# Gathering neighbour rows once per tile of 128 edges, into a ring, in all four edge stages

## The chip, the cores and the metric

The kernel runs on one core of a Trainium2 chip. The metric is the device time of one execution in microseconds (us), as the median of several runs. The engines are PE (TensorE; its weight loads are a row of their own, PEld), DVE (VectorE), ACT (ScalarE), POOL (GpSimd) and SP (SyncE, which only issues transfers and semaphore operations here). They run side by side and wait for each other by semaphores.

## What is computed

A graph of 12,500 nodes with 64 channels and 200,000 edges `src -> dst`, sorted by `dst`. Two CG convolutions, a layer norm, then two graph attention (GAT) convolutions, a batch norm behind each and a layer norm at the end, all in float32:

```python
def _cgconv(x, edge_index, Wf, bf, Ws, bs):
    z = concatenate([x[i], x[j]], axis=-1)          # i = dst, j = src
    m = sigmoid(z @ Wf + bf) * softplus(z @ Ws + bs)
    return x + segment_sum(m, i, num_segments=n)
...
def gat_conv(x, src, dst, edge_attr, W, We, att_s, att_d, att_e, bias):
    xl = x @ W                                      # self loops are added
    alpha = leaky_relu(a_src[src2] + a_dst[dst2] + a_edge, 0.2)
    ex = exp(alpha - segment_max(alpha, dst2)[dst2])
    p = ex / segment_sum(ex, dst2)[dst2]
    return segment_sum(xl[src2] * p[..., None], dst2) + bias
```

`dst` is drawn as the square of a uniform number, so that nodes with a low number have many edges and the last ones about 8 each.

## The kernel before, in words

**Tiles, blocks, steps.** The edges are cut into 1,563 tiles of 128, the nodes into 98 blocks of 128. A tile whose edges end in several blocks is visited once for each. Such a visit (tile, block) is a **step**: 1,658 steps are needed, padded to 1,664. Four steps are a **group** (416 groups), 128 steps a **batch** (13 batches, 32 groups each). `setup` works out which tile and which block each step has, and brings the edges' data into step order.

**Four edge stages.** `cg_edges` runs twice, `gat_edges` twice; between them stand `cg_tables`, `cg_finish`, `gat_tables` and `gat_finish`, each ended by a barrier of all engines. In an edge stage POOL gathers for each step the 128 source rows of its tile with one indirect DMA (`indirect_dma_start`; L677 for CG, from `q_table`, 128 words a row; L1134 for GAT, from `xl_table`, 65 words a row). Its loop is a fixed order of 1,664 gathers a stage, with one wait every four.

**CG.** For each group PE adds the gathered rows (L774, one 128x512 product with the identity) to the rows of the destination's table, which it picks with a one-hot matrix (L777, four products), and PE later sums the messages by destination (L787, four products). ACT works out logarithms and exponentials (L742 to L755), DVE the one-hot matrices (L577, L698), the messages and the accumulation (L724). The gathered rows stand in a ring of 4 groups, and POOL may refill a group when PE has done L777 on it.

**GAT.** Here POOL fills two buffers of a whole batch (128 rows of 65 words for each edge lane). Before a batch's messages can be weighed, its 128x128 scores must be complete: DVE adds the gathered score column, read with a strided view from the buffer, to the destination's part (L1189), which needs the whole batch landed; then come the segment maxima, their carries and the exponentials. This work on batch b+1 is laced into the 9 iterations (4 groups each) of the sums of batch b: the scores stand after iteration 1 on DVE (iteration 5 for the last batch). The sums are ACT's weighing (L1328, L1330), PE's products with the one-hot matrix (L1405) and DVE's accumulation (L1265). PE also spreads destination values two batches ahead (L1358, with the one-hot made by DVE in L1156 from `rel_rows`). SP fetches `rel_rows` for a pair of groups at a time (L655, L1105).

**The last batch.** When batch 11's sums reach iteration 5, DVE waits for batch 12's rows; its own sums then follow with no gather beside them.

## Time and profile before

| | us |
|---|---|
| median of 3 runs | 11,049.12 (11,041.77 to 11,055.13) |
| span of the profiled execution, first to last instruction | 9,392.2 |
| median less span: what lies around the span | 1,656.9 |

The page of the profile gives the span of the profiled execution and not its whole time, so what lies around the span is the difference to the median. The parts of the page show busy time by engine, the span in 40 slices, the costliest groups of instructions and what ended the idle time before them; the timeline shows single instructions with the engine's idle time before them in square brackets. A matmul of float32 stands as two records.

### The profile page before, as it was taken

Reading aid. Unit: us, or ns where it says so; the run is one execution under the profiler, and the core shown is the slowest. Engines: PE = TensorE matmul, PEld = TensorE weight load, DVE = VectorE, ACT = ScalarE, POOL = GpSimd, SP = SyncE. Lnnn points to the kernel's source line nnn. Section 1 sums busy time; section 2 is a strip of 40 time slices with the busy share of each in tenths; the row PEclk is TensorE's granted clock in tenths of the full one; section 3 lists DMA queues with packets and bytes.
Section 4 is the critical chain, followed back from the end, with each engine's and each line's share of the span. In section 5 each row is a group of like instructions: output and inputs, shape, how many; then the busy total and the mean of one; then the engine's idle time right before and its main releaser. Section 6 shows DMA issues by size and latency. Waiting matters only on the chain. (4 is left out here: it accounts for less than half of the span.)

```text
span 9392.2 us, 131283 instructions
## 1 busy us (share of the span) xinstructions
PE 5120.9 (55%) x26955; PEld 4302.7 (46%) x26956; DVE 4670.8 (50%) x14160; ACT 3046.4 (32%) x8219; POOL 6571.9 (70%) x6801
## 2 busy tenths in 40 slices
PE   2677777777677777777533253434552234343444
PEld 1555555555555555555423243434542234343443
DVE  6555555555555555555623353434552235353546
ACT  0444444444444444444302122222320122121222
POOL 2777777777577777777557777777716777777771
PEclk6888787788778887887655555555555555555555
DMA  4322223222222232222232232222203223222221
GB/s 134 91 76 77 76 75 76 75 77 77 82 77 77 75 76 77 77 75 76 68 76 53 45 59 50 56 52 52 49 11 75 45 49 59 46 58 49 58 44 30
DMA packets 436755, 612.92 MB, mean 65 GB/s; under 512 B 180134, under 2 KB 217754, under 8 KB 434779
## 3 DMA queue, kind: packets, MB, share of 16 engines
q0 software_dynamic: 214032, 332.71, 17.2%
q1 hardware_dynamic: 217116, 262.20, 10.3%
q10 hardware_dynamic: 5193, 13.44, 0.4%
q8 instruction: 144, 2.36, 0.1%
q14 instruction: 270, 2.21, 0.1%
HBM read 575.04 MB, written 32.78 MB: 65 GB/s over the span
## 5 line engine op out<-in xcount | busy, mean ns | idle before, releaser
L677 POOL DMA_INDIRECT big<-q_table,idx_stage x3328 | 3279.5, 985 | 1007.8 <-issue 930.3
L1134 POOL DMA_INDIRECT big<-xl_table,idx_stage x3328 | 3199.1, 961 | 1007.9 <-issue 985.3
L1405 PE MATMUL bank<-msg,onehot 128*128 128x66 f32 x6656 | 1597.3, 424 | 2227.4 <-DVE wide L1265 2003.0
L1405 PEld LDWEIGHTS bank<-msg,onehot 128*128 128x128 f32 x6656 | 1480.8, 328 | 2276.9 <-issue 2186.1
L774 PE MATMUL bank<-big,ident 128*128 128x512 f32 x1664 | 1216.8, 821 | 1236.0 <-DMA big<-q_table,idx_stage 1145.6
L777 PEld LDWEIGHTS bank<-big,wide 128*128 128x128 f32 x6656 | 1217.7, 257 | 574.9 <-issue 574.9
L777 PE MATMUL bank<-big,wide 128*128 x6656 | 1208.0, 342 | 0.0
L577 DVE TENSOR_TENSOR onehot<-iota,dst_rel 128x512 f32<-128x512 f32 x1664 | 1145.7, 689 | 2.9 <-issue 2.9
L705 DVE SCALAR_TENSOR_TENSOR work<-bank,work 128x256 f32<-128x256 f32 x832 | 352.3, 423 | 1459.7 <-ACT work L747 1456.2
L742 ACT ACTIVATE work<-bank 128x512 f32<-128x512 f32 x832 | 496.2, 596 | 1783.4 <-PE bank L777 1781.1
L1265 DVE TENSOR_TENSOR wide<-wide,bank 128x66 f32 x3328 | 739.4, 222 | 553.8 <-issue 182.6
L787 PEld LDWEIGHTS bank<-msg,onehot 128*128 128x128 f32 x6656 | 997.1, 229 | 4.3 <-DVE msg L713 3.9
L787 PE MATMUL bank<-msg,onehot 128*128 128x67 f32 (+1 forms) x6656 | 995.6, 302 | 3.9 <-DVE msg L713 2.4
L1189 DVE TENSOR_TENSOR work<-big,onehot_t 128x128 f32<-128x128 f32 x26 | 9.9, 379 | 1879.5 <-DMA big<-xl_table,idx_stage 1879.5
L724 DVE TENSOR_TENSOR wide<-wide,bank 128x67 f32 (+1 forms) x3328 | 735.3, 221 | 364.0 <-DVE wide L724 15.3
L774 PEld LDWEIGHTS bank<-big,ident 128*128 128x128 f32 x1664 | 297.7, 224 | 1338.4 <-DMA big<-q_table,idx_stage 691.2
L1328 ACT ACTIVATE msg<-work 128x8 f32<-128x8 f32 x448 | 94.5, 211 | 1533.6 <-PE bank L1405 1532.3
L747 ACT ACTIVATE work<-work 128x512 f32<-128x512 f32 x832 | 523.6, 629 | 103.4
L744 ACT ACTIVATE work<-work 128x512 f32<-128x512 f32 x832 | 523.7, 629 | 26.7
L1358 PEld LDWEIGHTS bank<-spread_bf,big 128*128 128x128 bf16 x3328 | 347.6, 147 | 340.3 <-issue 329.1
L1328 ACT ACTIVATE msg<-big 128x8 f32<-128x8 f32 x384 | 80.9, 211 | 1277.7 <-PE bank L1405 1258.8
L1330 ACT ACTIVATE msg<-big,work 128x64 f32<-128x64 f32 x1792 | 470.3, 333 | 0.0
(216 smaller groups left out, 4138.3 us busy)
## 6 DMA issues: line engine op xcount, KB each, us to landing
wide<-rel_rows SPq DMA_DIRECT2D x416, 256.0 KB, 3.4
big<-rel_rows SPq DMA_DIRECT2D x416, 256.0 KB
big<-q_table,idx_stage POOLq DMA_INDIRECT x3328
big<-xl_table,idx_stage POOLq DMA_INDIRECT x3328
q_table<-wide SPq DMA_DIRECT2D x12, 1024.0 KB, 5.2
edge_rows<-big SPq DMA_DIRECT2D x25, 257.0 KB, 6.6
xl_table<-big SPq DMA_DIRECT2D x12, 520.0 KB, 6.7
big<-in_edge_attr ACTq DMA_DIRECT2D x6, 1024.0 KB
```

The costliest lines, as they stand in the source:

```text
L577: return nc.vector.tensor_tensor(to, k.iota[:, :].unsqueeze(1).broadcast_to([P, GROUP, P]), k.dst_rel[:, ds(s, GROUP)].unsqueeze(2).broadc ...
L677: pool.indirect_dma_start(out=ring[:, u, s % GROUP, :], out_offset=None, in_=k.q_table, in_offset=bass.IndirectOffsetOnAxis(ap=k.idx_stage ...
L724: nc.vector.tensor_tensor(to, to, agg[c % UNROLL][:, i * P:i * P + width], ALU.add).then_inc(s_add if i < GROUP - 1 else s_acc, 1)
L742: nc.scalar.activation(soft[:, j], pre[j], ACT.Abs).then_inc(s_act, 1)
L744: nc.scalar.activation(soft[:, j], soft[:, j], ACT.Exp, scale=-1.0).then_inc(s_act, 1)
L747: nc.scalar.activation(soft[:, j], soft[:, j], ACT.Ln, bias=1.0).then_inc(s_ln, 1)
L774: nc.tensor.matmul(k.psum[j][:, :], k.ident[:, :], ring[:, j].rearrange("p i c -> p (i c)"), start=True, stop=False)
L777: last_one = nc.tensor.matmul(k.psum[j][:, i * P:(i + 1) * P], turned[:, j, i, :], p_tab[:, ds(at[i], 2 * C)], start=False, stop=i == GROU ...
L787: last_one = nc.tensor.matmul(agg[j][:, i * P:i * P + width], k.onehot[:, j, i, :], k.msg[:, j, i, 0:width], start=True, stop=True)
L1134: pool.indirect_dma_start(out=buf[p][:, s, :], out_offset=None, in_=k.xl_table, in_offset=bass.IndirectOffsetOnAxis(ap=k.idx_stage[:, s:s ...
L1265: nc.vector.tensor_tensor(to, to, sum_bank[c % UNROLL][:, i * P:i * P + C + 2], ALU.add).then_inc(e_add if i < GROUP - 1 else e_acc, 1)
L1405: last_one = nc.tensor.matmul(sum_bank[c % UNROLL][:, i * P:i * P + C + 2], k.onehot[:, c % UNROLL, i, :], k.msg[:, c % UNROLL, i, 0:C + 2 ...
```

## The change

Each edge tile is gathered once, and not once per step. A stage now gathers 1,568 tiles (392 groups of 4; `TGROUPS`) and POOL writes them in tile order into a **ring**: 32 tiles for CG, 256 for GAT. Which slot a step reads is no longer fixed in the code. `setup` makes three tables in `offsets`: the ring slot of each step (`RING_ROW`; GAT's is kept in DRAM until `gat_tables`), the tile group that each step group needs (`NEED_ROW`), and for each tile group the last step group that reads it (`LAST_ROW`). Engines read them into registers with `load_values`.

SP becomes a **relay**: in tile order it waits until the readers are done with an older group (`s_used`), raises `s_free`, waits for the group's landing and raises `s_land`. POOL waits for `s_free` (in GAT also for `s_land`), PE for `s_land`. The fetch of `rel_rows` moves from SP to ACT. The indices are no longer brought into step order. In CG the identity product is split into four of 128 columns, each with a slot from a register. In GAT the score column can't be read with one strided view any more; PE copies it with 128 products of the identity by one column (`far_scores`), before DVE's scores, and ACT reads each slot by a register.

```diff
+TGROUPS = 8 * -(-TILES // (8 * GROUP))
+TAIL_TILES = TGROUPS * GROUP - TILES // P * P
+LANES = 8
...
+CG_RING = 32
+GAT_RING = 2 * P
+AHEAD = 4
...
             for row, width in ((ACC_ROW, AW), (TAB_ROW, 2 * C), (SPREAD_ROW, 2 * PARTS)):
-                link(nc.vector.tensor_scalar(k.offsets[row:row + 1, :], b_row, float(NB - 1), float(width), ALU.min, ALU.mult))
+                link(nc.vector.tensor_scalar(k.offsets[row:row + 1, 0:STEPS], b_row, float(NB - 1), float(width), ALU.min, ALU.mult))
+            link(nc.vector.tensor_scalar(clipped, b_row, float(NB - 1), None, ALU.min))
+            link(nc.vector.tensor_tensor(tile_int, iota_s[0:1, :], clipped, ALU.subtract))
+            link(nc.vector.tensor_scalar(k.offsets[RING_ROW:RING_ROW + 1, 0:STEPS], tile_int, CG_RING - 1, 7, ALU.bitwise_and, ALU.logical_shift_left))
+            link(nc.vector.tensor_scalar(gat_ring, tile_int, GAT_RING - 1, None, ALU.bitwise_and))
+            nc.vector.tensor_scalar(gat_ring, gat_ring, float(TW), None, ALU.mult).then_inc(s_ring, 1)
...
+def relay(k, sp, s_used, s_land, s_free, depth, row_base):
+
+
+    def turn(it, freeing):
+        before = it * LANES + (AHEAD - depth)
+        if any(freeing):
+            last = load_values(k, sp, LAST_ROW, before + (STEPS + freeing.index(True)), freeing.count(True), 1, GROUPS)
+        for j in range(LANES):
+            if freeing[j]:
+                sp.wait_ge(s_used, last[j - freeing.index(True)])
+                sp.sem_inc(s_free, 1)
+            sp.wait_ge(k.rows[j], it * (16 * GROUP) + (16 * GROUP + row_base))
+            sp.sem_inc(s_land, 1)
...
-                        wait(pool, s_X, b * BGROUPS + (s // GROUP - UNROLL + 1))
+                        wait(pool, s_free, b * BGROUPS + (g - CG_DEPTH + 1))
...
+                    slot = load_values(k, pe, RING_ROW, step, GROUP, 0, (CG_RING - 1) * 2 * C)
+                    need, = load_values(k, pe, NEED_ROW, it * CG_UNROLL + (STEPS + c), 1, 1, TGROUPS)
+                    pe.wait_ge(s_land, need)
                     wait(pe, s_softs, n[c - 3])
-                    nc.tensor.matmul(k.psum[j][:, :], k.ident[:, :], ring[:, j].rearrange("p i c -> p (i c)"), start=True, stop=False)
+                    for i in range(GROUP):
+                        nc.tensor.matmul(k.psum[j][:, i * P:(i + 1) * P], k.ident[:, :], ring[:, ds(slot[i], 2 * C)], start=i == 0, stop=False)
...
             if layer == 0:
+                sp.dma_start(k.offsets[RING_ROW:RING_ROW + 1, 0:STEPS], k.gat_ring_row).then_inc(s_ring, 16)
+                sp.wait_ge(s_ring, 16)
...
                     if s % GROUP == 0:
...
+                        wait(pool, s_free, b * BGROUPS + (g - GAT_DEPTH + 1))
                         pool.sem_inc(s_turn, 1)
...
+                        wait(pool, s_land, b * BGROUPS + (g - LANES + 1))
...
-                for half in range(2):
-                    v.wait_ge(s_gat[p][half], turn * (16 * HALF) + (16 * HALF + gat_base[p][half]))
-                link(nc.vector.tensor_tensor(x3[:, 0, :], gather[:, :, C], near_sb[:, :, 0], ALU.add))
+                v.wait_ge(s_far, b + 1)
+                link(nc.vector.tensor_tensor(x3[:, 0, :], k.psum[5][:, 0:P], near_sb[:, :, 0], ALU.add))
...
+            def fetch(pair, q):
+                wait(act, a_T, 2 * (pair - PAIRS) + 2 if not isinstance(pair, int) or pair >= PAIRS else 0)
+                act.sem_inc(s_fetch, 1)
+                act.dma_start(rel_pair[q], rel_row(k, pair)).then_inc(s_rel[q], 16)
...
+                        slot = load_values(k, act, RING_ROW, b * P + s, GROUP, 0, (GAT_RING - 1) * TW)
...
+                            last_one = nc.scalar.activation(k.msg[:, c, i, 0:C], ring[:, ds(slot[i], C)], ACT.Copy, scale=wsw[p][:, s + i, 0:1])
...
+            def far_scores(b):
+                wait(pe, s_fe, 2 * b)
+                for c in range(0, BGROUPS, 2):
+                    slot = load_values(k, pe, RING_ROW, b * P + c * GROUP, 2 * GROUP, 0, (GAT_RING - 1) * TW)
+                    need, = load_values(k, pe, NEED_ROW, b * BGROUPS + (STEPS + c + 1), 1, 1, TGROUPS)
+                    pe.wait_ge(s_land, need)
+                    for i in range(2 * GROUP):
+                        at = c * GROUP + i
+                        last_one = nc.tensor.matmul(k.psum[5][:, at:at + 1], k.ident[:, :], ring_score[:, ds(slot[i], 1)], start=True, stop=True)
+                last_one.then_inc(s_far, 1)
...
                 for it in range(BIT + 1):
                     sums(it, it == 0, it == BIT)
+                    if not ends(b) and it == (5 if late(b) else 1):
+                        far_scores(b + 1)
```

Three places show what stands on the engines. First PE in a CG stage, a group's forming (ISA rows are register work for an address). Before, from the end of one group's sums on (L583 loads offsets, L774 is the identity product, L777 the one-hot products):

```order
L583 TENSOR_LOAD offsets
L774 MATMUL bank<-big,ident 128x512 [waits cge0_soft_s,rows3]
L777 ISA [waits cge0_onehot_t]
L777 MATMUL bank<-big,wide 128x128
L777 ISA
L777 MATMUL bank<-big,wide 128x128
```

Now, from the same point on (L622 is the old load, L630 the new ones, L851 the split identity product):

```order
L622 TENSOR_LOAD offsets
L630 TENSOR_LOAD offsets x2
L851 ISA [waits cge1_soft_s,cge1_landed]
L851 MATMUL bank<-wide,ident 128x128
L851 ISA
L851 MATMUL bank<-wide,ident 128x128
L851 ISA
L851 MATMUL bank<-wide,ident 128x128
L851 ISA
L851 MATMUL bank<-wide,ident 128x128
L854 ISA [waits cge1_onehot_t]
```

Two register loads are added ahead of the wait for the rows, and one product became four with a register address each; the one-hot products follow as before.

Second PE in a GAT stage between iterations 1 and 2 of a batch's sums. Before, the spreading of a group (L1358) is followed directly by the next group's sums (L1405):

```order
L1358 ISA
L1358 MATMUL bank<-spread_bf,big 128x6
L70 REGISTER_ALU
L1405 MATMUL bank<-msg,onehot 128x66 [waits gat0_e_e_acc,gat0_e_e_onehot,gat0_e_e_msg]
L1405 MATMUL bank<-msg,onehot 128x66 x3
```

Now the first of 16 blocks of `far_scores` stands there (L1440 is the spreading, L1457 the product by one column):

```order
L1440 ISA
L1440 MATMUL bank<-spread_bf,big 128x6
L79 ISA
L630 ISA [waits gat0_e_factor]
L630 TENSOR_LOAD offsets
L630 ISA
L630 TENSOR_LOAD offsets
L1457 ISA [waits gat0_e_landed]
L1457 MATMUL bank<-big,ident 128x1
L1457 ISA
L1457 MATMUL bank<-big,ident 128x1
```

Between two groups of PE's sums stand 128 products, 32 register loads and 16 waits for landings; the sums come behind them.

Third ACT in a GAT stage, the weighing of a group (L1328 and L1330 before). Before:

```order
L1328 ACTIVATE msg<-big 128x4x2 [waits gat0_e_e_agg]
L1330 ACTIVATE msg<-big 128x64 x4
L1328 ACTIVATE msg<-big 128x4x2 [waits gat0_e_e_agg]
L1330 ACTIVATE msg<-big 128x64 x4
L1328 ACTIVATE msg<-big 128x4x2 [waits gat0_e_e_agg]
```

Now (L1369 is the fetch of `rel_rows`, every second group):

```order
L1399 ACTIVATE msg<-big 128x64
L1369 DMA big<-rel_rows 128x1024 [waits gat0_e_a_onehot_t]
L630 TENSOR_LOAD offsets
L1397 ACTIVATE msg<-big 128x4x2 [waits gat0_e_e_agg]
L1399 ISA
L1399 ACTIVATE msg<-big 128x64
```

ACT gained a register load and four register addresses for each group, and for each second group a transfer with a wait for DVE's one-hot.

## Rows read from the trace of the kernel before

**Rows 1.** The page: span, part 1, PEclk in 40 slices

```profile
span 9392.2 us, 131283 instructions
PE 5120.9 (55%) x26955; PEld 4302.7 (46%) x26956; DVE 4670.8 (50%) x14160; ACT 3046.4 (32%) x8219; POOL 6571.9 (70%) x6801
...
PEclk6888787788778887887655555555555555555555
```

**Rows 2.** Page part 5: count, busy us, mean ns, idle us before

```profile
L677 POOL DMA_INDIRECT big<-q_table,idx_stage x3328 | 3279.5, 985 | 1007.8 <-issue 930.3
L1134 POOL DMA_INDIRECT big<-xl_table,idx_stage x3328 | 3199.1, 961 | 1007.9 <-issue 985.3
```

**Rows 3.** Lines L677 and L1134, POOL: duration min/median/max ns, first and last start

```profile
L677 POOL DMA_INDIRECT big<-q_table,idx_stage x3328: 940/946/3329, 254.2 to 4621.6; - x196
L1134 POOL DMA_INDIRECT big<-xl_table,idx_stage x3328: 940/945/1458, 4745.8 to 9178.2; - x196
```

**Rows 4.** Timeline, POOL: first and last gather of GAT stage 1

```profile
4745.75 0.97 POOL L1134 DMA_INDIRECT big<-xl_table,idx_stage  x1 [0.81 <-POOL idx_stage L1136]
...
6855.73 0.94 POOL L1134 DMA_INDIRECT big<-xl_table,idx_stage  x1 [0.31 <-issue]
```

**Rows 5.** Timeline, PE: a CG group at the low, then at the high clock

```profile
2003.54 2.07 PE L774 MATMUL bank<-big,ident 128*128 128x512 f32 x2 [2.05 <-DMA big<-q_table,idx_stage]
2005.40 1.81 PE L777 MATMUL bank<-big,wide 128*128 x8
...
2008.64 1.12 PE L774 MATMUL bank<-big,ident 128*128 128x512 f32 x2 [0.59 <-DMA big<-q_table,idx_stage]
2009.60 1.05 PE L777 MATMUL bank<-big,wide 128*128 x8
```

**Rows 6.** Timeline, DVE: waits for a batch's rows, batches 2, 10, 11, 12

```profile
5233.08 0.38 DVE L1189 TENSOR_TENSOR work<-big,onehot_t 128x128 f32<-128x128 f32 x1 [76.71 <-DMA big<-xl_table,idx_stage]
...
6532.05 0.38 DVE L1189 TENSOR_TENSOR work<-big,onehot_t 128x128 f32<-128x128 f32 x1 [66.56 <-DMA big<-xl_table,idx_stage]
...
6693.93 0.38 DVE L1189 TENSOR_TENSOR work<-big,onehot_t 128x128 f32<-128x128 f32 x1 [67.77 <-DMA big<-xl_table,idx_stage]
...
6858.67 0.38 DVE L1189 TENSOR_TENSOR work<-big,onehot_t 128x128 f32<-128x128 f32 x1 [39.18 <-DMA big<-xl_table,idx_stage]
```

**Rows 7.** Line L583, PE's register loads: duration ns min/median/max

```profile
L583 PEldq TENSOR_LOAD <-offsets x1664: 326/332/517, 260.2 to 9085.6; - x185
```

**Rows 8.** CG, GAT stage 1: us, PE PEld DVE ACT POOL busy, PEclk, DMA

```profile
254.00:2420.00 2166.00, 1543.06 (x7488) 1203.33 (x7488) 1234.69 (x3747) 985.16 (x2081) 1643.73 (x1690) 0.81 0.29 76
...
4746.00:6859.00 2113.00, 819.20 (x4852) 786.44 (x4852) 834.41 (x2801) 453.39 (x1943) 1607.52 (x1690) 0.50 0.27 53
```

**Rows 9.** Timeline, PE: products by one column in GAT stage 1

```profile
6881.41 0.58 PE L1381 MATMUL bank<-ones_row,big 1*128 1x1 f32 x2
6881.86 0.56 PE L1382 MATMUL bank<-ones_row,big 1*128 1x1 f32 x2
```

**Rows 10.** Timeline, PE: the stop in batch 10's sums

```profile
6698.84 1.52 PE L1405 MATMUL bank<-msg,onehot 128*128 128x66 f32 x6 [72.68 <-DVE wide L1265]
```

**Rows 11.** Line L655, SP's transfers: issue to landing

```profile
DMA to landing us min/median/max: 3.0/3.4/4.3
```

**Rows 12.** Timeline, DVE in setup: the step tables; POOL's first gather there

```profile
48.40 1.88 DVE L390 TENSOR_TENSOR wide<-wide 1x1664 f32<-1x1664 f32 x1
50.31 3.12 DVE L393 TENSOR_SCALAR offsets<-wide 1x1664 int32<-1x1664 f32 x3
...
83.80 5.97 POOL L268 DMA_INDIRECT wide<-edge_rows,work  x1 [78.70 <-DMA edge_rows<-big]
```

**Rows 13.** Lines L961 and L520: duration ns min/median/max; window of L961's stage

```profile
L961 PE MATMUL bank<-gw,work x392: 417/418/477, 4702.6 to 7059.4; 64*128 64x66 f32 x196
L520 PE MATMUL bank<-small,work x784: 271/272/579, 215.5 to 2462.4; 64*128 64x128 f32 x196
...
4700.00:4745.00 45.00, 36.12 (x245) 30.75 (x245) 13.52 (x32) 12.66 (x27) 0.24 (x1) 0.50 0.57 88
```

More of the change, by code:

```diff
@@ L586, in load_offsets, with load_values @@
     return values
+def load_values(k, eng, row, first, count, low, high):
+    _, values = k.nc.values_load_multi_w_load_instructions(
+        k.offsets[row:row + 1, ds(first, count)], engines=[eng.engine], min_val=low, max_val=high,
+        skip_runtime_bounds_check_because="setup makes them so")
+    return values
+def relay(k, sp, s_used, s_land, s_free, depth, row_base):
[9 more added lines that the diff above has]
+            sp.sem_inc(s_land, 1)
+    whole = -(-(depth - AHEAD) // LANES)
+    for it in range(whole):
+        turn(it, [it * LANES + j >= depth - AHEAD for j in range(LANES)])
+    with sp.Fori(whole, TGROUPS // LANES) as it:
+        turn(it, [True] * LANES)
 def counts(eng, first, lo, hi):
@@ L637, in cg_edges @@
     at = CG_PAIRS * GROUP * P
[L638 removed]
+    ring = k.wide[:, at:at + CG_RING * 2 * C]
     soft = k.work[:, 0:UNROLL * GROUP * P].rearrange("p (u i c) -> p u i c", u=UNROLL, c=2 * C)
@@ L649, in _, with batch @@
             k.clear_old(sp)
-            def fetch(it):
-                for q in range(CG_PAIRS):
-                    wait(sp, s_T, (it - 1) * CG_UNROLL + 2 * q + 2 if not isinstance(it, int) or it else 0)
-                    sp.sem_inc(s_turn, 1)
-                    sp.dma_start(rel[q], rel_row(k, it * CG_PAIRS + q)).then_inc(s_rel[q], 16)
-            fetch(0)
-            with sp.Fori(1, CG_ITERS) as it:
-                fetch(it)
+            relay(k, sp, s_X, s_land, s_free, CG_DEPTH, row_base)
         @block.gpsimd
         def _(pool):
-            def batch(b):
-                for s in range(P):
-                    u = s // GROUP % UNROLL
+            def batch(b, tiles):
+                for s in range(tiles):
+                    g = s // GROUP
                     if s % GROUP == 0:
-                        wait(pool, s_X, b * BGROUPS + (s // GROUP - UNROLL + 1))
+                        wait(pool, s_free, b * BGROUPS + (g - CG_DEPTH + 1))
                         pool.sem_inc(s_turn, 1)
-                    if s % HALF == HALF // 2:
+                    if s % HALF == HALF // 2 and tiles == P:
                         start = b * P + (HALF if s < HALF else P)
@@ L758, in iteration @@
                     stages(u, first, last, (3, sigmoids), (2, logs))
-            pipelined(act, CG_ITERS, iteration)
+            for q in range(CG_PAIRS):
+                fetch(q, q)
+            iteration(0, True, False)
+            with act.Fori(1, CG_ITERS - 1) as it:
+                iteration(it, False, False)
+            iteration(CG_ITERS - 1, False, False)
+            iteration(CG_ITERS, False, True)
         @block.tensor
@@ L1349, in batch @@
                     weights(b + 1, 1 - p)
-            over_batches(act, batch)
+            for pair in range(BGROUPS // 2 + PAIRS):
+                fetch(pair, pair % PAIRS)
+            batch(-1, 1, -1)
+            batch(0, 0, 0)
+            with act.Fori(0, OUTER - 2) as j:
+                batch(j * 2 + 1, 1, j)
+                batch(j * 2 + 2, 0, j + 1)
+            for b in range(NBATCH - 4, NBATCH):
+                batch(b, b % 2, b // 2)
         @block.tensor
```

158 lines of the change are left out of this document (90 added, 68 removed).

## The prediction

> **What bounds the kernel now.** I read the page first: POOL is busiest with 70% of the span, the others lie at 32 to 55% [rows 1]. Then POOL's gathers. In each edge stage it issues 1,664 of them; the idle time before them, 1,007.8 us over 3,328, is 0.303 us each, put down to its own issuing, and no wait: POOL is back to back [rows 2]. A gather's median is 945 to 946 ns [rows 3], with the dispatch 1.249 us. The mean is 985 ns in CG and 961 ns in GAT [rows 2]: 0.040 and 0.016 us more each, or 67 and 27 us a stage, which comes and goes while POOL waits for nobody. GAT stage 1 shows the sum: first gather at 4,745.75, last at 6,855.73, which is 2,110.0 us, or 1.268 us a gather [rows 4].
>
> Everybody else waits for the rows. In CG, PE's idle time before L774 is ended by the gather (2.05 and 0.59 us in two groups) [rows 5]. In GAT, DVE stands still 66.6 to 76.7 us in each batch before L1189, until a batch's rows are there [rows 6]. Neighbouring batches lie 161.9 us apart (6,532.05 to 6,693.93), of which 67.8 is that wait: the work between two landings takes 94.1 us, at most 97 in other batches. The last one differs: from 6,693.93 to 6,858.67 is 164.7 us with a wait of only 39.2, so its work is 125.6 us, since the scores stand later in the sums there. So GAT has 66 us of slack in most batches and 39 in the last.
>
> **What the change removes.** 96 gathers a stage (1,664 less 1,568) at the median pitch of 1.249 us: 119.9 us. I take the median and not the mean, because I leave the 67 and 27 us of longer gathers in the stage: the other engines' work is still 1,664 steps. Of the 392 tile groups the readers need 391 (1,563 tiles), so the last group's four gathers, 5.0 us, fall beside other work.
>
> **CG, two stages.** PE gets two more register loads per group, 0.33 us each [rows 7], and four register addresses. They stand ahead of the wait for the rows, where PE idles anyway. A group of steps takes 4 x 1.289 = 5.16 us now and would take 119.9 / 416 = 0.29 less, 4.87 us. The split product moves the same columns; one-hot products of that shape take 1.05 us a group of four at the high clock against 1.12 for the one wide product, 1.81 against 2.07 at the low one [rows 5]: no loss, taken at nothing. ACT and DVE are busy for 0.46 and 0.57 of the stage [rows 8], so 6% more speed is there; ACT's transfer per two groups is hidden by its idle half. POOL's ring is deeper (8 groups, not 4) and the relay lets it run ahead of the readers, so I book no stall. The relay's own handing on I book at 0.5 us once, at the end. Saving: 119.9 + 5.0 - 0.5 = 124.4 us a stage, **249 us** for both. Bounds: 0 (PE can't follow, below) and 125.
>
> **GAT, two stages.** Added on PE are 128 products by one column a batch. The nearest rows are one-column products: L1381 starts at 6,881.41, L1382 at 6,881.86 [rows 9], 0.45 us; the eight records of L1405 and L777 at the low clock go at 0.213 us each, two records a product, 0.427 us, and I take that: 128 x 0.427 = **54.6 us a batch**. At the high clock the pitch of L777's records is 0.11 us (1.05 us for eight, with the tail) [rows 5], which gives 28.5 us: the lower bound. The register loads (32 a batch, 0.33 us [rows 7]) and the addresses run in PE's sequencer ahead of the array; I take them as hidden behind the products, and the upper bound has them in series.
>
> Where does this lie? PE reaches `far_scores` one group (about 2.2 us) ahead of the stop that starts now at 6,698.84 - 72.68 = 6,626.16 [rows 10], and DVE can't go on without it. Most of the 128 products find their rows landed and fill the stop. So a batch now lasts the longer of two things: its gathers, or 94 to 97 us of old work plus 54.6 less 2.2, about 147.6 us. The sorted `dst` of the inputs gives the tiles that each batch of steps ends on: 127, 253, 378, 501, 624, 745, 865, 985, 1,103, 1,220, 1,337, 1,453, 1,562. At 1.268 us a tile a batch takes 161 us at first and 147 to 148 us in batches 9 to 11: the gathers still win, by a hair. Scores of batch 11 then start 1,453 x 1.268 + 3 (landing [rows 11], a transfer from another queue) + 3.4 (the last 8 products) + 1 = 1,850 us into the stage. For the last batch the work is 125.6 - 2.2 + 54.6 = 178 us, while its 110 tiles take 140: here **the work wins**, and batch 12's scores start at 2,028 us. Before, that was 6,858.67 - 4,745.75 = 2,112.9 [rows 4, 6]. Saving 85 us a stage where the gathers alone would give 124; the other 39 us are the new products with no cover. The sums of batch 12 behind it are unchanged but for ACT's register loads, which its waits for PE hide; I book 1 us. So 84 us, **168 us** for both.
>
> ACT now waits with each second group for DVE's one-hot (L1156) before it issues the fetch of `rel_rows`. Behind it on ACT stands the next group's weighing, for which PE waits. DVE accumulates four groups late, so this costs ACT its lead and not the pace: nothing. POOL's second wait per group falls into the 0.30 us of dispatch: nothing, with 0.1 us x 392 = 39 us a stage as the other bound.
>
> **Setup and tables.** DVE's table chain gets five operations over 1,664 elements of one partition: one like L390 (1.88 us) and four like L393 (3.12 / 3 = 1.04) [rows 12], 6.0 us, and about eight short ones, 3 us. Everything behind them in setup hangs on DVE (POOL's first gather waits 78.7 us for its stores [rows 12]): 9 us, nothing hides it. The ring table goes out to DRAM and comes back, each 3.0 to 3.4 us [rows 11], of which the return is bare: 3 us. Together **12 us** lost (bounds 5 and 20).
>
> **Sum.** -249 - 168 + 12 = -405 us on the profiled execution's span: 9,392 to 8,987. The page doesn't show that execution's whole time; what lies around the span is taken as it was, 1,656.9 us, so the median goes from 11,049.1 to **10,644 us**.
>
> [...] The loads: the rows show 0.33 us for a register load of four values. [...]
>
> **Rivals.**
> 1. *The products are slow (slower than before).* If a register load or address can't run ahead of the array, each of the 16 blocks costs 3.4 us of products plus two loads (0.66), eight addresses and a wait, some 2.0 us: 87 us a batch instead of 54.6. Then the work wins from batch 2 on (at 488 us): 488 + 9 x (95 - 2.2 + 87) + (123.4 + 87) = 2,317 us for batch 12's scores, 204 us later than before in each GAT stage. Median 10,644 + 2 x 288 = 11,220. It decides from F, the cost of a batch's `far_scores`: the start is 1,447 + 10 F, so a GAT stage gains nothing from F = 67 us on (median 10,812), and the whole change nothing from F = 78. For it: nothing in the trace has two loads among products. Against: L583's loads run while products of the group before are under way.
> 2. *The high clock comes.* F = 28.5 us: batch 12's scores at 1,848 + 123.4 + 28.5 = 2,000 us, 28 us a stage better: 10,588.
> 3. *CG's readers can't follow.* At the low clock a CG group costs PE three times 1.7 to 1.9 us, 5.2 us, more than the 4.87 that the gathers would leave; at the high clock 2.9. The granted clock is 0.81 [rows 8], so both occur. If the shorter waits don't bring the high clock more often, or relay and loads add to each group, CG keeps its time: 10,644 + 249 = 10,893, or part of the way.
> 4. *The change saves gathers but no time*, since SP's in-order relay releases rows later than POOL can deliver them, in all stages: 11,060. Against: SP has two waits a group and nothing else to do.
>
> **Chances.** Forecast 0.53; rival 1 in full 0.09; GAT gains next to nothing (F 62 to 72) 0.11; rival 2 0.12; rival 3 0.12; rival 4 0.03. The range from 10,560 (all gathers covered, 10,563) to 10,830 (GAT stages gain nothing, plus the bounds of setup) leaves out rivals 1 and 4 and the full form of 3. About 0.2% is what a measurement of this kernel can tell from no change: faster by more 0.88, within 0.03, slower 0.09.
>
> **What would show it.** 1,568 gathers a stage, pitch 1.27 to 1.29 us, idle before each still 0.30. CG windows about 124 us shorter. In GAT, L1457's records at 0.21 us; DVE's wait for `far_scores` in each batch; batches 149 to 161 us apart and the last about 178. Wrong would be: waits ahead of POOL's gathers, a GAT batch longer than 165 us, L1457 at another pitch, or PE waiting for `s_land` in CG with the rows long there.

## The result and the profile after

The changed kernel takes **12,258.42 us** (median of 4 runs, 12,256.23 to 12,263.07) against 11,045.44 us before (median of 4, 11,038.50 to 11,055.13): ratio 1.110, 95% interval 1.108 to 1.111. The forecast was 10,644 us, faster by 4%. Direction and size are wrong.

The page of the kernel after, its span, TensorE's row of part 1, and the granted clock in 40 slices:

```profile
span 12256.2 us, 173779 instructions
PE 6901.5 (56%) x38616; PEld 6518.7 (53%) x38617; DVE 4643.4 (38%) x14173; ACT 3046.5 (25%) x8220; POOL 6237.3 (51%) x6409
...
PEclk6777777777777777755555555555555555555555
```

POOL was busy for 70% of the span before [rows 1] and is for 51% now. The span also tells something on its own: it is 2 us shorter than the time of its execution (12,258.15). Before, span and time were 1,657 us apart.

What ended POOL's idle time before its gathers, in the attention stages (L1200) and in the convolution stages (L736); the columns are us in total and how many times:

```profile
L1200 POOL DMA_INDIRECT big<-xl_table,idx_stage x3136: 938/944/1482, 5370.1 to 11913.3; - x196
...
  SPq L648: 1940.4, 120
  issue: 1028.3, 2972
```

```profile
L736 POOL DMA_INDIRECT wide<-q_table,idx_stage x3136: 938/944/4581, 255.4 to 5231.0; - x196
...
  issue: 877.8, 2783
  SPq L646: 821.2, 351
```

Before, POOL waited for nobody [rows 2]. Now it waits for the relay on SP 1,940 us in the attention stages and 821 us in the convolution stages. A gather itself still takes 944 ns, where [rows 3] has 945 to 946. The relay is only the messenger (L648 raises a landing, which SP reaches only after L646). Its own waits before L646, where it hands a freed group on, were ended by the readers, above all by ACT's last reading of a group in the attention stages (L1399) and by PE's last product on one in the convolution stages (L854); "remote" is a release whose sender the trace doesn't name (waits of SP in the kernel after; us in total, times, longest):

```profile
SPq L646 <- ACT msg L1399: 4113.6, 365, 130.1
SPq L646 <- remote: 3141.0, 350, 24.4
SPq L646 <- PE bank L854: 1381.7, 358, 14.9
```

Two starts of the first score operation in the timeline of DVE in the kernel after (start, us, and in brackets the idle time before and what ended it):

```profile
6410.10 0.29 DVE L1253 TENSOR_TENSOR work<-bank,near_sb 128x128 f32<-128x128 f32 x1 [56.32 <-PE bank L1457]
...
6656.58 0.29 DVE L1253 TENSOR_TENSOR work<-bank,near_sb 128x128 f32<-128x128 f32 x1 [74.74 <-PE bank L1457]
```

These rows answer to [rows 6]. Two batches are 246.5 us apart, where the forecast had 149 to 161. DVE waits 74.7 us of them for `far_scores` (L1457), and 171.8 us go into the rest, where [rows 6] gave 94. Over batches 2 to 11 of both stages the means are 245.9 us, of which 59.6 are that wait and 186.4 the rest. The 128 products themselves stand in 54.7 to 54.8 us in 11 of the 26 batches, as forecast, and are drawn out to as much as 83.5 us in others. The larger surprise is the work around them, which takes nearly twice its time.

A hint of why stands in the timeline of PE in a convolution stage of the kernel after:

```profile
1438.83 0.83 PE L854 MATMUL bank<-big 128*128 x6
1440.63 0.27 PE L854 MATMUL bank<-big 128*128 x1 [0.96 <-issue]
1441.36 0.36 PE L854 MATMUL bank<-big 128*128 x1 [0.47 <-issue]
1442.78 1.09 PE L864 MATMUL bank<-msg,onehot 128*128 128x67 f32 x8 [1.06 <-issue]
```

In the middle of a group, with nothing to wait for, PE goes over to one array operation in 0.7 us and back. From 750 to 2,250 us this happens close to a hundred times, and PE's idle time before its products that is put down to "issue" adds up to 467 us there, against 8 us in the same window of a2_after_u16 (an experiment below). Register operations show the same on other engines. Counted over all of the trace's records, the register, branch and semaphore operations that took 650 to 760 ns (their median is 17 to 57 ns, by engine) are:

```
kernel, its time            PE   ACT    DVE    SP   POOL
before,  9,391 us            3     0      0     0      0
after*,  9,009 us            4     0      0     0      0
before*, 11,083 us         307     0  1,872   634      0
after,  12,258 us          559   838  1,101   118      0
```

The first three rows are runs of the experiments below (e0_before, a2_after_u16, b10_before_bursts); the star marks kernels that differ slightly from the two compared. The profile shown ahead of the prediction has 3, 0, 0, 0, 0, like the first row.

### The profile page after: what moved, and what is told of

It is laid out like the page before. It is cut to its first block and busy times, and to the rows that moved or that the text cites. A ratio compares the mean times of both kernels' runs of the same rounds, so it can differ in the third digit from the quotient of the medians.

```text
span 12256.2 us, 173779 instructions
## 1 busy us (share of the span) xinstructions
PE 6901.5 (56%) x38616; PEld 6518.7 (53%) x38617; DVE 4643.4 (38%) x14173; ACT 3046.5 (25%) x8220; POOL 6237.3 (51%) x6409
## 3 DMA queue, kind: packets, MB, share of 16 engines
q0 software_dynamic: 201536, 312.86, 11.7%
## 5 line engine op out<-in xcount | busy, mean ns | idle before, releaser
L1200 POOL DMA_INDIRECT big<-xl_table,idx_stage x3136 | 2999.0, 956 | 3031.4 <-SPq L648 1940.4
L736 POOL DMA_INDIRECT wide<-q_table,idx_stage x3136 | 3131.9, 999 | 1700.7 <-issue 877.8
L851 PE MATMUL bank<-wide,ident 128*128 x6656 | 1370.2, 343 | 992.1 <-issue 959.6
L851 PEld LDWEIGHTS bank<-wide,ident 128*128 128x128 f32 x6656 | 1133.8, 243 | 1113.8 <-issue 1099.5
L1457 PE MATMUL bank<-big,ident 128*128 x6656 | 1425.6, 350 | 195.4 <-issue 187.9
L1457 PEld LDWEIGHTS bank<-big,ident 128*128 128x128 f32 x6656 | 1431.6, 332 | 190.0 <-issue 189.7
L854 PE MATMUL bank<-big 128*128 x6656 | 1238.6, 334 | 374.9 <-issue 371.3
L854 PEld LDWEIGHTS bank<-big 128*128 128x128 f32 x6656 | 1119.2, 246 | 418.8 <-issue 417.8
L1440 PEld LDWEIGHTS bank<-spread_bf,big 128*128 128x128 bf16 x3328 | 346.4, 140 | 1184.9 <-issue 1177.5
L1440 PE MATMUL bank<-spread_bf,big 128*128 x3328 | 318.3, 178 | 1160.2 <-issue 972.4
L1222 DVE TENSOR_SCALAR big<-big,iota_col 128x512 bf16<-128x512 bf16 x832 | 310.9, 378 | 1029.0 <-issue 336.2
```

The costliest lines, as they stand in the source:

```text
L736: pool.indirect_dma_start(out=ring[:, s % CG_RING * 2 * C:(s % CG_RING + 1) * 2 * C], out_offset=None, in_=k.q_table, in_offset=bass.Indir ...
L851: nc.tensor.matmul(k.psum[j][:, i * P:(i + 1) * P], k.ident[:, :], ring[:, ds(slot[i], 2 * C)], start=i == 0, stop=False)
L854: last_one = nc.tensor.matmul(k.psum[j][:, i * P:(i + 1) * P], turned[:, j, i, :], p_tab[:, ds(at[i], 2 * C)], start=False, stop=i == GROU ...
L1200: pool.indirect_dma_start(out=ring[:, slot * TW:(slot + 1) * TW], out_offset=None, in_=k.xl_table, in_offset=bass.IndirectOffsetOnAxis(ap= ...
L1440: last_one = nc.tensor.matmul(near[:, ds(column + (c * GROUP + i) * SLOT, 2 * PARTS)], turned[:, c % UNROLL, i, :], spread_bf[:, ds(at[i], ...
L1457: last_one = nc.tensor.matmul(k.psum[5][:, at:at + 1], k.ident[:, :], ring_score[:, ds(slot[i], 1)], start=True, stop=True)
```

## Experiments

Sums of stages are from the first gather of one stage to the first of the next. In all but one version of the changed kernel a mask of ten bits is laid over each value that an engine waits for (`need & 1023`, `last[...] & 1023`), one register operation more for each wait.

**Where the 1,657 us lie** (e0_before, no edit).

> The kernel before, unchanged. Its profiled span was 9,392.2 us while its runs take 11,038 to 11,055; the changed kernel's span (12,256.2) and its time (12,258.2) differ by 2 us. Theory A (the 1,657 us lie outside the span, before the first or after the last instruction): the span comes out at 9,392 again. Theory B (the profiled execution of before ran under other conditions than its timed ones): the span comes out near 11,045, and its trace shows where the 1,653 us stand.

Measured: 9,391.17 us with a span of 9,389.4. Neither theory had it: the span is 9,390 again, but so is the time. On this chip the kernel before takes 9,391 us, and 1.8 us lie around the span. So the profile shown ahead of the prediction and the runs shown with it (11,049) are of two conditions in which the same program takes different times. The text calls them two kinds of chip; whether it is the chip or something that comes and goes on one, no run here tells, since no chip was seen in both. All comparisons below are therefore with before on the same chip.

**Parts of the change, one at a time.** e1_before_pe_loads, with the load of one value beside that of four:

```diff
+ load_offsets(k, pe, TAB_ROW, ..., GROUP, 2 * C)
+ load_offsets(k, pe, TAB_ROW, ..., 1, 2 * C)
- nc.tensor.matmul(k.psum[j][:, :], k.ident[:, :], ring[:, j]...)
+ for i in range(GROUP):
+     nc.tensor.matmul(k.psum[j][:, i * P:(i + 1) * P], k.ident[:, :], ring[:, j, i, :], start=i == 0, stop=False)
```

> The kernel before with what the change adds to TensorE in the convolution stages alone: two more register loads per step (of four values and of one) and the identity product of 512 columns as four of 128. Nothing is left out. Theory 1 (TensorE's instruction stream, 164 records between two stalls in the trace of after, is what makes the convolution stages longer): both stages grow, by up to the 297 us each by which the stages of after are longer than those profiled before; 11,045 + up to 594. Theory 2 (the relay on the sync engine holds GpSimd back): no change, 11,045 within 0.3%.

Measured: 9,378.35 against 9,385.36. The values of the added loads are not used, and the trace has no load more than before (1,664 on TensorE): what ran is the split product alone (4,992 matmul records more), and it costs nothing that a single run can show. e2 and e3 are single runs too.

e2_before_act_fetch: `fetch` of the relative positions in ScalarE's program, as in the diff of the change, and none on SyncE.

> The kernel before with the fetches of the relative positions issued by ScalarE, as in the changed kernel, in all four edge stages. Nothing is left out. If the fetch's place is a cause, the time rises by 50 us or more; the prediction's own step (hidden, at nothing) says 11,045 within 0.3%.

Measured: 9,385.41 against 9,385.36. The place of the fetch costs nothing.

e3_after_cg_whole:

```diff
- slot = load_values(k, pe, RING_ROW, step, GROUP, 0, (CG_RING - 1) * 2 * C)
- for i in range(GROUP):
-     nc.tensor.matmul(..., k.ident[:, :], ring[:, ds(slot[i], 2 * C)], start=i == 0, stop=False)
+ nc.tensor.matmul(k.psum[j][:, :], k.ident[:, :], p_tab[:, 0:GROUP * 2 * C], start=True, stop=False)
```

> The changed kernel with a mask on the values that are waited for (one register operation a wait) and, in the convolution stages, the identity product whole (one of 512 columns, from a fixed place, so the gathered rows do not enter the sums) and without the load of the four slots. The attention stages are as in the changed kernel. Theory 1 (TensorE's stream in the convolution stages): about 300 us a stage come back, 12,258 - 600 = 11,660. Theory 2 (the relay): the stages stay at 2,444 us each, 12,258 within 1%.

Measured: 9,010.42 against 9,385.36. Far from both numbers, since these stood on 12,258. Beside a0_after_masked (9,007, the next run) it says that the 832 slot loads and the split product cost nothing in the changed kernel.

**The changed kernel on other chips.** a0_after_masked (masks only) and a2_after_u16, where the values waited for are read as the low 16 bits of their entries. It has as many instructions on every engine as the changed kernel, but for 178 register operations more on SyncE.

> The changed kernel with one register operation (a mask) ahead of each wait on a value read from a table; nothing is left out. On the chip of the first four runs the kernel before took 9,385 us, not 11,045, and a version of the changed kernel with lighter convolution stages 9,010. Theory A (the changed kernel loses by its own work on any chip): the ratio to before is 1.11 here too, near 10,400 where before takes 9,385. Theory B (the result comes from a condition of the chip in which TensorE issues one array operation in 0.7 us for stretches of 3 to 8 us, and the prediction's mechanism holds where it is absent): 9,000 to 9,050 where before takes 9,385, ratio 0.96; 12,258 or a little more where before takes 11,045.

Measured: 9,007.36 us against 9,389.54, ratio 0.959 (0.957 to 0.961).

> The changed kernel instruction for instruction (as many rows on each engine), where the values that are waited for are read as the low 16 bits of their table entries, in place of the masks. It asks whether the masks of the other runs hide the loss. If the loss belongs to the unmasked program, the ratio to before is 1.11 on this chip too; if it belongs to the chip's condition in the recorded comparison, 9,000 to 9,010 where before takes 9,385 (the masks cost nothing), ratio 0.96, and 12,258 within 0.3% where before takes 11,045.

Measured: 9,008.51 us against 9,394.53, ratio 0.959 (0.958 to 0.961). So the masks hide nothing, and on these chips the changed kernel is **faster by 4.1%**. A third chip gave the same:

> The same kernel as a0_after_masked, on whatever chip this call gets. Where before takes 9,385 us: 9,007 within 0.3%. Where before takes 11,045 us: by the theory that this condition of the chip is what turned the sign, 12,258 within 1% (the masks add one register operation a wait); by the theory that the unmasked program itself is the slower one, 9,007 x 11,045 / 9,385 = 10,600.

Measured: 9,018.07 against 9,397.93, ratio 0.960 (0.957 to 0.963).

The page of a2_after_u16, what ended POOL's idle time before its gathers in the attention and the convolution stages, and three starts of the score operation:

```profile
span 9005.4 us, 173957 instructions
PE 6420.8 (71%) x38616; PEld 6158.7 (68%) x38617; DVE 4671.9 (52%) x14173; ACT 3016.6 (33%) x8220; POOL 6226.0 (69%) x6409
...
PEclk6888888888788888888655555555555555555555
```

```profile
L1203 POOL DMA_INDIRECT big<-xl_table,idx_stage x3136: 940/944/1457, 4502.6 to 8742.9; - x196
...
  issue: 924.8, 3057
  SPq L651: 20.4, 67
```

```profile
L739 POOL DMA_INDIRECT wide<-q_table,idx_stage x3136: 940/945/4584, 261.3 to 4375.0; - x196
...
  issue: 942.9, 3117
  SPq L649: 5.2, 17
```

```profile
5455.54 0.29 DVE L1256 TENSOR_TENSOR work<-bank,near_sb 128x128 f32<-128x128 f32 x1 [56.44 <-PE bank L1460]
...
5609.09 0.29 DVE L1256 TENSOR_TENSOR work<-bank,near_sb 128x128 f32<-128x128 f32 x1 [53.31 <-PE bank L1460]
...
6541.32 0.29 DVE L1256 TENSOR_TENSOR work<-bank,near_sb 128x128 f32<-128x128 f32 x1 [52.03 <-PE bank L1460]
```

POOL is back to back: its waits for the relay (L649 and L651 together) are 23 us in the attention and 5 us in the convolution stages; batches lie 153.6 us apart, of which 53.3 is the wait for the far products and 100.2 other work. Against the trace of e0_before, stage by stage: setup +3.9, convolutions -115.6 and -127.3, attentions -72.7 and -72.3, together -384.0 us, all of the difference of the spans.

**The cover of the far products.** x2_no_far and x4_far_twice:

```diff
 # x2_no_far
- slot = load_values(k, pe, RING_ROW, b * P + c * GROUP, 2 * GROUP, 0, (GAT_RING - 1) * TW)
- for i in range(2 * GROUP):
-     last_one = nc.tensor.matmul(k.psum[5][:, at:at + 1], k.ident[:, :], ring_score[:, ds(slot[i], 1)], ...)
+ last_one = nc.tensor.matmul(k.psum[5][:, at:at + 2 * GROUP], k.ident[:, :], k.ident[:, 0:2 * GROUP], ...)
 # x4_far_twice
+     nc.tensor.matmul(k.psum[5][:, at:at + 1], k.ident[:, :], ring_score[:, ds(slot[i], 1)], ...)
      last_one = nc.tensor.matmul(k.psum[5][:, at:at + 1], k.ident[:, :], ring_score[:, ds(slot[i], 1)], ...)
```

> The changed kernel (masked waits) whose far_scores issues one product of eight columns in place of eight products of one column with their slot load, 16 times a batch; so the scores lack the far term. Where before takes 9,385 us: the prediction's step (the products are hidden behind the gathers in all batches but the last) says that only the last batch of each attention stage gets shorter, by the 54.8 us that its products take, two stages, 110 us: 9,007 - 110 = 8,897, and that no other batch changes, since GpSimd sets their pitch. Where before takes 11,045: if the stalls of 0.7 us follow the number of instructions that an engine is given, 3,072 fewer products and 416 fewer loads give back more than the 110 us, by several hundred; if they follow time alone, 12,258 - 110 = 12,150.

Measured: 8,919.14 (before 9,395.20): 88 us less than a0, where 110 were expected. In the last batch the distance between scores falls from 179.3 to 151.7 us and not by the full 54.8: without the products DVE still waits 24 us there. The batch before it falls from 148.5 to 142.3, so the products were not wholly covered in that one.

> The changed kernel (masked waits) with each product of far_scores issued twice; nothing is left out. It asks where the cover ends. Where before takes 9,385 us: a batch becomes the longer of its gathers (147 to 161 us) and 94 to 97 + 2 x 54.8 - 2.2 = 202 us; 11 batches grow by some 45 us and the last by 55, 550 us a stage: 9,007 + 1,100 = 10,107. If instead the products were hidden altogether (theory of free products), 9,007. Where before takes 11,045: 12,258 + at least 110 x 13 = 13,700.

Measured: 10,127.74 (expected 10,107), slower than before. A batch in its DVE timeline, 203 to 207 us from the next:

```profile
6043.44 0.29 DVE L1253 TENSOR_TENSOR work<-bank,near_sb 128x128 f32<-128x128 f32 x1 [108.02 <-PE bank L1458]
```

Both sides of the cover are where the sum had them, within some 10 us a stage: once is hidden in nearly all but the last batch, twice is not. A batch is the longer of its gathers and (other work + far products), with 95 to 100 us of other work on these chips.

**A better last batch?** v1_far_split:

```diff
- if not ends(b) and it == (5 if late(b) else 1):
-     far_scores(b + 1)
+ if late(b) and it in (3, 4, 5):
+     far_scores(b + 1, *{3: (0, 12), 4: (12, 20), 5: (20, BGROUPS)}[it])
+ if not ends(b) and not late(b) and it == 1:
+     far_scores(b + 1)
```

> The changed kernel (masked waits) with the last batch's far_scores in three parts: 6 blocks of 8 products after iteration 3 of the sums before it, 4 after iteration 4, 6 after iteration 5, where all 16 stood after iteration 5; nothing is left out. In the trace of the masked kernel TensorE starts these products at 6,494.5, when the rows of nearly all blocks have landed, and DVE gets the scores at 6,549.4. If the other engines' work hides the earlier blocks, the last batch's scores come up to 34 us earlier in both attention stages: 9,007 - 68 = 8,940. TensorE is busy for 1.7 of the 1.95 us of each step of the sums there, so the rival says that the products only change places: 9,007 - 10. In either case it beats before (9,385) where before takes that.

Measured: 8,998.00 us, ratio 0.958 (0.957 to 0.960) to before; 9 us from a0, no more than the spread of its runs. The rival was right. DVE's last wait in the first attention stage fell from 52.0 to 21.5 us, and its other time in that batch grew from 127.3 to 153.5.

**The relay.** e5_ring16:

```diff
-CG_RING = 32
+CG_RING = 16
-AHEAD = 4
+AHEAD = 2
```

> The changed kernel (masked waits) with a ring of 16 tiles in the convolution stages in place of 32, and a relay that hands on a freed group two groups ahead of a landing in place of four; nothing is left out. It prices the relay. Where before takes 9,385 us: a group of the ring has to come free, be gathered (4 x 1.25 us), land and be read within four groups' time, 4 x 4.9 = 19.6 us, which the trace of the masked kernel leaves room for: 9,007 + 0 to 30. If the relay's handing on is a bottleneck (the rival on the relay), GpSimd waits in both stages and they grow by 100 us or more. Where before takes 11,045: TensorE's stalls of 3 to 9 us have half the ring to cover them, so more than 12,258.

Measured: 9,003.04 (before 9,397.93). POOL's waits for the relay in the convolution stages grow from 2 (a0) to 112 us, and the time doesn't change.

> The same kernel as e1_before_pe_loads, for a chip on which before takes 11,045 us. If the call's chip is one where before takes 9,385, it takes 9,378 to 9,390 again and says only that this holds from chip to chip. If before takes 11,045 there: by the theory that the stalls of 0.7 us come with the instructions an engine is given, the 9,984 further products' records and 3,328 loads of TensorE in the convolution stages add 200 us or more; by the theory that they come with time alone, it stays at 11,045.

Measured: 9,384.91 against 9,393.61, ratio 0.999 (0.998 to 1.000). Its chip was one of the faster kind; it says nothing new.

**On a chip of the slower kind.** The last three kernels add `burst(k, pe)`, ten unused register loads, ahead of each fourth group on TensorE.

> The kernel before with ten register loads in a row on TensorE (some 0.35 us each, 3.5 to 4 us a burst) ahead of every fourth step in all four edge stages, like the stalls of 3 to 9 us in the trace of after; nothing is left out. Where before takes 9,385 us: a batch of the attention stages has 66 us of slack and gets 9 x 4 = 36 us of bursts: hidden, but for the last batch (39 us of slack); the convolution stages have 30% of TensorE's time free: hidden. 9,385 + 0 to 80. If TensorE's pauses cannot be hidden (rival): 4 us x 104 x 2 + 36 x 26 = 1,770 more.

> The changed kernel (masked waits) with the same bursts; nothing is left out. By the theory that the far products used up the slack of the attention batches, so that any pause of TensorE now lengthens them: a batch's work grows from 148 to 184 us, over the 152 to 157 us of its gathers: 11 x 30 + 36 = 366 us a stage, 9,007 + 730 = 9,740, slower than before with the same bursts. By the rival (the changed kernel is no more sensitive than the kernel before), the difference of 382 us between the two stays.

> x2_no_far (the scores lack the far term: one product of eight columns in place of eight products, 16 times a batch) with the same bursts. By the theory it has the slack of the kernel before again: 8,919 + 0 to 100. By a rival in which the relay, the loads of the slots or the fetches on ScalarE make the changed kernel sensitive, it grows by several hundred like b11.

Again the unused loads are not in the program: the traces have the loads of before, and 102 register operations more. So the three are, but for these, the kernel before, a0_after_masked and x2_no_far; the intended test of pauses was not made. But they ran on a chip where before takes 11,057.32 us, the only one of six that was of this kind. Each of the three is a single run; that of b11 lies 0.5% above the four runs of the changed kernel at 12,258:

```
                            9,385 us kind    11,057 us kind
before                      9,391            11,083 (b10)
changed, masks              9,007            12,322 (b11)
changed, no far products    8,919            11,117 (b12)
```

The far products, with the slot loads that go with them, cost 88 us on one kind and **1,205 us** on the other, and without them the changed kernel is about level with before there (11,117 against 11,083). They are what turns a kernel that gains nothing into one that loses 11%. Rows of b10 (page, one start of the score operation, the attention gathers' waits):

```profile
span 11081.7 us, 131385 instructions
...
L1273 DVE TENSOR_TENSOR wide<-wide,bank 128x66 f32 x3328 | 740.0, 222 | 2136.4 <-issue 1251.0
```

```profile
6473.73 0.38 DVE L1197 TENSOR_TENSOR work<-big,onehot_t 128x128 f32<-128x128 f32 x1 [1.00 <-issue]
...
6679.57 0.38 DVE L1197 TENSOR_TENSOR work<-big,onehot_t 128x128 f32<-128x128 f32 x1
```

```profile
L1142 POOL DMA_INDIRECT big<-xl_table,idx_stage x3328: 938/944/1462, 5481.2 to 10806.6; - x196
...
  issue: 990.1, 3121
  ACT msg L1338: 722.7, 172
```

and a batch's start in b11 and in b12:

```profile
6433.93 0.29 DVE L1261 TENSOR_TENSOR work<-bank,near_sb 128x128 f32<-128x128 f32 x1 [57.87 <-PE bank L1465]
```

```profile
6251.96 0.29 DVE L1261 TENSOR_TENSOR work<-bank,near_sb 128x128 f32<-128x128 f32 x1 [11.57 <-PE bank L1463]
```

The wait of 66 to 77 us of [rows 6] has gone: in the kernel before, on this chip, DVE starts the scores of batches 2 to 11 almost at once (0.1 to 6.2 us idle before them), these batches lie 186 to 206 us apart (197.5 in the mean, where e0_before has 162.4), and it is POOL that waits for the sums (L1338, 723 us). DVE's accumulation (L1273) stands idle for 2,136 us, 1,251 of them put down to "issue"; the same operation in e0_before, on the faster kind:

```profile
L1265 DVE TENSOR_TENSOR wide<-wide,bank 128x66 f32 x3328 | 738.6, 222 | 553.3 <-issue 182.5
```

With 196 us of other work against 161 us of gathers there is no cover, and a batch of the changed kernel is 186 + 60 = 246 us. Without the products (b12) it is 188 + 14 = 202.

Set against e0_before, b10 is longer by 371.6 and 361.4 us in the convolution stages and by 474.4 and 478.3 in the attention stages. That is where the slower kind puts its 1,692 us. The stages, b10 against the recorded trace of after (with no masks): setup -8.7, convolutions -55.1 and -47.3, attentions **+627.5 and +658.1**, together +1,174.5, the whole difference of the spans. The convolution stages gain on this chip too, 102 us together; the attention stages lose more than twelve times as much, 1,286. Of the first +627.5, 484 stand between the scores of batches 1 and 12. The other 143 come earlier, before the scores of batch 1: from the stage's first gather on, PE passes some 156 records of the spreading products in 360 us where b10 took 200 and a2 54 for as many, most of it at 0.7 us an operation. b12 has such a start too, 53 us longer than b10's, so these 53 us are not the far products' and their cause stays open; they are most of the 63 to 67 us by which b12's attention stages are still longer than b10's.

## Why the prediction was wrong

- **The failed step** is the last line of the sum: "what lies around the span is taken as it was, 1,656.9 us". 1.8 us lie around the span of e0_before, and 1.8 around that of b10_before_bursts (11,081.7 of 11,083.45), which has the longer time. The 1,657 us were inside the executions that were timed, and the profile shown was of another kind of execution, without them. Every slack read from it held for one kind of chip, and the time was forecast for the other. The step that this spoiled is the attention batch: "94 to 97 us of old work" was 186 us in the kernel after (196 in b10), so the 54.6 us of products had no 66 us of waiting to fill.
- **POOL back to back in all edge stages** [rows 2]: right on the faster kind (925 us of "issue" and 23 of waits for the relay over the 3,136 gathers of the attention stages in a2), wrong on the slower one, where POOL waits 723 us for the sums already in the kernel before.
- **Convolutions, -124.4 us each**: -115.6 and -127.3 on the faster kind (e0 to a2), -55.1 and -47.3 on the slower. Split product, slot loads, ACT's fetch at nothing: e1, e2, e3 agree. Ring and relay at nothing: e5 agrees, on the faster kind. On the slower kind more than half of the saving is lost, as in rival 3; POOL waits 821 us for groups to come free. The runs don't say how much of that is rival 3's low clock (0.75 granted from 750 to 2,250 us of after, 0.85 in a2) and how much PE's pauses of 467 us there.
- **Attentions, -84 us each**: -72.7 and -72.3 on the faster kind. F = 54.6 us a batch: 54.8 measured where nothing is in between (11 of 26 batches in a2 and in after), up to 83.5 in after. Batches of 149 to 161 us: 148 to 159, and the last 179 for 178. Scores of batch 12 at 2,028 us into the stage: 6,541.3 - 4,502.6 = 2,038.7. That "the gathers still win, by a hair" did not hold in the late batches: those of a2 alternate between 148.5 and 153 us where the gathers alone would take 147 to 148, and in x2, without the products, batch 11's scores stand at 1,848 us, next to the 1,850 of the sum, against 1,859 in a2. The term that was mis-sized on the slower kind is the old work. The longer of 161 and 186 + 60 is 246; the formula stands, its input was that of another condition.
- **The register loads**, taken at 0.33 us each: those of eight values took 0.76 us and those of one value 0.47 (a2), some 20 us a batch and not 10.6. They stayed hidden behind the products, as assumed.
- **Setup, +12 us**: +3.9 in the traces of e0 and a2. Too high, though setup itself spreads over several us: 254.2 to 258.5 in the traces of before on the faster kind, 256.8 to 265.9 in those of the changed kernel.
- **Sum, -405 us on 9,392**: -384.0 in the traces, and -382 in the medians of a0 and before. All of the forecast's terms hold within 23 us together, on the faster kind of chip.
- **Rival 1** gave the right sign (11,220) by a mechanism that did not occur: its loads and addresses did not hold the products up (54.8 us a batch in a2), their cover went. That the two come out on the same side is luck. **Rival 2** (the high clock comes, F = 28.5 us) did not occur: the granted clock in the attention stages stays low (5 in the PEclk rows, 0.50 over 4,700 to 6,300 us of a2), also through 54.8 us of products without a gap (0.50 and PE busy throughout from 6,486 to 6,541 us of a2). **Rival 4** had the picture (POOL waits for SP's relay) and, at 0.03, the wrong cause: a relay can only hand on what has been used.
- **The missing rival**: 15% between a profile's span and the time of the runs is more than any term of the sum. "The timed executions have 1,657 us that this trace doesn't show; if a quarter of them lie in the attention batches (16 us each of 26), the work passes the gathers" could have been worked out from [rows 6]: the 13 us between gathers and work (161 - 148) were all there was. In fact more than half of them lay in the attention stages.

**What stays open** is what the 0.7 us are, and whether they belong to a chip or to its condition at the time. They come on PE, ACT, DVE and SP and in no register operation of POOL (0 in all four rows of the count). The gathers' queue does not take more time of the DMA engines on the slower kind (part 3, share of 16 engines' span, kernel after and then a2_after_u16):

```profile
q0 software_dynamic: 201536, 312.86, 11.7%
```

```profile
q0 software_dynamic: 201536, 312.86, 16.8%
```

11.7% of 12,256 is 1,434 us and 16.8% of 9,005 is 1,513. Fetching of code is not shown as the cause either: in the kernel after not one packet of the two instruction queues (q8 and q14) falls between 750 and 2,250 us, where PE's pauses of 467 us stand. In the convolution stages PE's pauses (two or more of its records in a row that start 650 to 760 ns apart) begin 100 to 200 of its records apart in 182 of 262 cases of the kernel after and in 152 of 198 of b10, with medians of 165 and 159 among these. That looks as if they followed the amount of work given to the engine; but at the start of the attention stage of the kernel after, from 5,387 to 5,704 us, PE pauses nearly without a break. The reading of instructions and the writing of the trace's own records are the author's guesses; no run here shows either as the cause, or says why one chip of six does it.

## What to carry to other kernels

Before a slack is read from a trace, set the trace's span against the time of the runs: where they differ by more than the terms of the sum, as here by 1,657 us against 405, the trace can be of another condition, and each slack needs a second value. A change that moves work into a wait can count only on the wait's smallest value over the chips on which the kernel will run: here 0.1 to 6.2 us (b10), where the profile of the other kind showed 66 to 77 [rows 6]. Here the gathering by tiles in the convolution stages gained on both kinds of chip (243 and 102 us), while 128 one-column products a batch in the attention stages gained only where the wait existed.

## What the runs showed of the hardware

- The same program takes 9,385 to 9,398 us on five chips and 11,057 us on a sixth, with the same 944 ns for a gather (median, e0 and b10) and 222 ns for an accumulation of the attention stages (mean, L1265 and L1273), and with register, branch and semaphore operations that go from medians of 17 to 57 ns, by engine, to 650 to 760 ns in stretches (2,813 of these in b10, 3 in e0).
- On TensorE a register load of four values takes 0.34 us at L622 and 0.50 at L630, one of eight values 0.76 and one of a single value 0.47 us (medians of such loads in after and a2; L630's own median of 0.49 mixes the three). Leaving 832 of them out of the convolution stages (e3) changed the time by 3 us, which is within the spread.
- SyncE's load of eight values took 0.53 us from neighbouring 32-bit words, and 1.65 us as 16-bit values two apart (a2_after_u16), at no cost to the whole (9,009 against 9,007).
- One-column products with a 128 x 128 load each go at 0.43 us a product at a granted clock of 0.50 (54.8 us for 128, a2 and after), on both kinds of chip where no pause falls among them.
